# Cross attention with LayerNorm: row sums on VectorE, another order of the last tiles, x added by TensorE for the last two outputs

## The reference

```python
qs = (q @ wq).reshape(Bq, Lq, H, HD).transpose(0, 2, 1, 3)      # q is x
ks_ = (k @ wk)...; vs = (v @ wv)...                             # k and v are the context
scores = einsum('bhqd,bhkd->bhqk', qs, ks_) / sqrt(HD)
scores = where(mask, -inf, scores)
attn_w = softmax(scores, axis=-1)
out = (attn_w @ vs) @ wo + q
mu, var = mean(out), mean((out - mu) ** 2)
out = (out - mu) / sqrt(var + EPS) * gamma + beta
```

## Time and profile before

| | us |
|---|---|
| three runs, median (lowest to highest) | 640.73 (640.59 to 640.79) |
| the profiled execution | 641.83 |
| its span | 640.0 |
| TensorE busy, share of the span | 614.0, 96% |
| VectorE busy | 513.8, 80% |
| ScalarE busy | 523.8, 82% |
| POOL busy | 494.9, 77% |
| mean granted clock of TensorE, share of full speed | 0.991 |

### The profile page before, as it was taken

One profiled execution on the slowest core, in us unless ns is written; L12 is line 12 of the kernel. 1 busy time (PEld: TensorE's weight loads), 2 busy tenths in 40 slices (PEclk: granted clock), 3 DMA queues, 4 the chain that ended last, 5 costly groups with the idle time before them and its releaser, 6 DMA issues.

```text
span 640.0 us, 12593 instructions
## 1 busy us (share of the span) xinstructions
PE 614.0 (96%) x3816; PEld 485.2 (76%) x3816; DVE 513.8 (80%) x989; ACT 523.8 (82%) x1718; POOL 494.9 (77%) x639
## 2 busy tenths in 40 slices
PE   7988999999999999999999999999999999999885
PEld 5755687887878788787878878787878878786654
DVE  5844588888889888888879988887888988787787
ACT  4888998888878888897887988887988888789860
POOL 6475558797978979797987979797897879578674
PEclk9999899999999999999999999999999999999998
DMA  8450212222231232122231212232122221411103
GB/s 285 155 178 15 76 34 83 84 86 80 99 110 50 100 99 96 55 98 100 75 123 63 99 63 90 96 99 100 52 99 72 94 68 67 165 45 66 40 17 132
DMA packets 34786, 57.76 MB, mean 90 GB/s; under 512 B 6816, under 2 KB 7840, under 8 KB 34720
## 3 DMA queue, kind: packets, MB, share of 16 engines
q1 hardware_dynamic: 34720, 56.96, 26.4%
HBM read 39.53 MB, written 16.78 MB: 88 GB/s over the span
## 4 chain that ended last, share of the span: by engine, by line
PE 76%; DVE 10%; ACT 9%; issue 2%; SPq 1%; DMA 1%; POOLq 0%; POOL 0%; DVEq 0%; ACTq 0%
PE bank L384 24%; PE bank L308 22%; PE bank L331 14%; PE bank L341 7%; ACT pr L490 6%; PE bank L362 4%; DVE pr L628 2%; PE bank L367 2%; DVE nm L634 2%; PE bank L345 2%; PE bank L301 1%; DMA ptr<-xT 1%; DVE sm L642 1%; ACT ptr L456 1%; DVE kl L599 1%
## 5 line engine op out<-in xcount | busy, mean ns | idle before, releaser
L488 ACT ACTIVATE pr<-pr,nm 128x77 f32<-128x77 f32 x864 | 228.0, 347 | 52.3 <-DVE nm L634 50.3
L788 POOL TENSOR_TENSOR pn<-pr,rec 128x512 f32<-128x512 f32 x128 | 135.3, 1057 | 95.3 <-DVE rec L644 87.5
L628 DVE SCALAR_TENSOR_TENSOR pr<-msk,bank 128x308 f32<-128x308 uint8 x256 | 109.4, 469 | 41.2 <-PE bank L331 40.6
L634 DVE TENSOR_REDUCE nm<-pr 128x8 f32<-128x616 f32 x128 | 101.8, 795 | 4.4
L308 PE MATMUL bank<-xh,wqh 128*128 128x512 f32 x256 | 103.3, 403 | 1.3 <-DVE ql L616 1.3
L384 PE MATMUL bank<-woh,ah 128*128 128x512 f32 x256 | 101.8, 398 | 1.1 <-DVE al L651 1.1
L384 PE MATMUL bank<-woh,al 128*128 128x512 f32 x256 | 101.2, 395 | 0.0
L384 PE MATMUL bank<-wol,ah 128*128 128x512 f32 x256 | 101.1, 395 | 0.0
L308 PE MATMUL bank<-xh,wql 128*128 128x512 f32 x256 | 100.9, 394 | 0.0
L308 PE MATMUL bank<-xl,wqh 128*128 128x512 f32 x256 | 100.4, 392 | 0.0
L456 ACT ACTIVATE ptr<-bank 128x512 f32<-128x512 f32 (+1 forms) x256 | 95.3, 425 | 2.9 <-PE bank L341 2.8
(11 more groups left out here) (69 smaller groups left out, 1139.8 us busy)
## 6 DMA issues: line engine op xcount, KB each, us to landing
xraw<-xT SPq DMA_DIRECT2D x59, 256.0 KB, 3.0
xres<-x SPq DMA_DIRECT2D x58, 256.0 KB, 2.7
out<-y SPq DMA_DIRECT2D x56, 256.0 KB, 2.0
wk_sb<-wk SPq DMA_DIRECT2D x4, 256.0 KB, 4.1
wq_raw<-wq SPq DMA_DIRECT2D x4, 256.0 KB, 6.2
wv_sb<-wv SPq DMA_DIRECT2D x1, 1024.0 KB, 8.7
wo_raw<-xT SPq DMA_DIRECT2D x4, 256.0 KB, 8.8
wo_raw<-wo SPq DMA_DIRECT2D x1, 1024.0 KB, 5.4
```

The lines of the kernel that those rows point to most:

```text
L488: last = nc.scalar.activation(s, s, ACT.Exp, bias=nm[:, t % 2, h:h + 1], scale=1.0)
L628: nc.vector.scalar_tensor_tensor(out=pr[:, 4 * g:4 * g + 4, :], in0=msk[:, b % 2, t % TB, :].unsqueeze(1).broadcast_to([P, 4, LK]), scalar ...
L634: nc.vector.tensor_reduce(nm[:, t % 2, HH * half:HH * half + HH], pr[:, HH * half:HH * half + HH, :], AX.X, ALU.max, negate=True).then_inc ...
L788: nc.gpsimd.tensor_tensor(pn[:, half, 0:4, :].rearrange("p s (e k) -> p (s e) k", e=2), pr[:, hs, 0:KM], rec[:, t % 2, hs].unsqueeze(2).br ...
```

## The change

Three things are changed.

- `SUMS` is gone: in all tiles the exponentials have no accumulator, and `row_sums` on VectorE reduces the eight sums before it takes the reciprocals.
- The order of the last tiles is another one on all four computing engines. SyncE's program is as it was.
- For outputs 62 and 63 (`XADD = T - 2`) TensorE adds x: an fp32 matmul of x with the identity opens the accumulation in a bank, and the twelve matmuls of the output projection go on top of it. The banks are the two score banks SB, and the matmul waits until the last mask operation has read them and until x has arrived. `residual` of these outputs takes mean and variance straight from the bank, and `finish_1` reads the bank.

```diff
-SUMS = (6, T - 4)
+XADD = T - 2
...
-        misc += [("o", T - 10), ("o", T - 9), ("v", E - 3), ("o", T - 8), ("o", T - 7), ("o", T - 6), ("v", E - 2), ("o", T - 5),
-                 ("o", T - 4), ("v", E - 1), ("o", T - 3), ("o", T - 2), ("o", T - 1)]
+        misc += [("o", T - 10), ("o", T - 9), ("v", E - 3), ("o", T - 8), ("o", T - 7), ("o", T - 6), ("v", E - 2),
+                 ("o", T - 5), ("o", T - 4), ("o", T - 3), ("v", E - 1)]
+        def out_bank(o):
+            return SB[o % 2] if o >= XADD else misc_bank(("o", o))
...
+            def add_x(t):
+                pe.wait_ge(d_xe, 16 * (T - VFIN))
+                pe.wait_ge(v_st, NG * T - 1 + t % 2)
+                nc.tensor.matmul(out_bank(t)[:], ident[:], z_of(t), start=True, stop=False)
...
             project_o(T - 10)
             transpose_p(T - 5, 0)
             scores(T - 4, (2, 3))
+            scores(T - 3, (0, 1))
             project_o(T - 9)
             transpose_p(T - 5, 1)
-            scores(T - 3, (0, 1))
+            scores(T - 3, (2, 3))
             weigh_v(E - 3)
-            scores(T - 3, (2, 3))
+            scores(T - 2, (0, 1))
             transpose_p(T - 4, 0, after=E - 3)
             project_o(T - 8)
             transpose_p(T - 4, 1)
-            scores(T - 2, (0, 1))
             project_o(T - 7)
             transpose_p(T - 3, 0)
             scores(T - 2, (2, 3))
+            transpose_p(T - 3, 1)
             project_o(T - 6)
-            transpose_p(T - 3, 1)
             scores(T - 1, (0, 1))
+            scores(T - 1, (2, 3))
             weigh_v(E - 2)
             project_o(T - 5)
-            scores(T - 1, (2, 3))
             transpose_p(T - 2, 0, after=E - 2)
             transpose_p(T - 2, 1)
             project_o(T - 4)
+            add_x(T - 2)
+            add_x(T - 1)
             transpose_p(T - 1, 0)
+            project_o(T - 3)
             transpose_p(T - 1, 1)
             weigh_v(E - 1)
-            project_o(T - 3)
             project_o(T - 2)
             project_o(T - 1)
...
-                    if SUMS[0] <= t < SUMS[1]:
-                        last = nc.scalar.activation(s, s, ACT.Exp, bias=nm[:, t % 2, h:h + 1], scale=1.0)
-                    else:
-                        last = nc.scalar.activation(s, s, ACT.Exp, bias=nm[:, t % 2, h:h + 1], scale=1.0,
-                                                    accum_out=sm[:, t % 2, h:h + 1])
+                    last = nc.scalar.activation(s, s, ACT.Exp, bias=nm[:, t % 2, h:h + 1], scale=1.0)
...
-                if SUMS[0] <= t < SUMS[1]:
-                    nc.vector.tensor_reduce(sm[:, t % 2, hs], pr[:, hs, :], AX.X, ALU.add).then_inc(v_sum, 1)
-                    dve.wait_ge(v_sum, n - 2 * SUMS[0])
+                nc.vector.tensor_reduce(sm[:, t % 2, hs], pr[:, hs, :], AX.X, ALU.add).then_inc(v_sum, 1)
+                dve.wait_ge(v_sum, n)
...
+                if o >= XADD:
+                    nc.vector.bn_stats(st[:, e], out_bank(o)[:]).then_inc(v_bs, 1)
+                    dve.wait_ge(v_bs, o + 1)
+                    nc.vector.bn_aggr(mv[:, e], st[:, e]).then_inc(v_bn, 1)
+                    return
```

More of the change, by code:

```diff
@@ L370, in weigh_v @@
                     mm.then_inc(p_pv, 1)
+            def add_x(t):
+                pe.wait_ge(d_xe, 16 * (T - VFIN))
+                pe.wait_ge(v_st, NG * T - 1 + t % 2)
+                nc.tensor.matmul(out_bank(t)[:], ident[:], z_of(t), start=True, stop=False)
             def project_o(t):
                 r = t % 4
-                misc_free(pe, ("o", t))
-                o = misc_bank(("o", t))
-                n = 0
+                if t < XADD:
+                    misc_free(pe, ("o", t))
+                o = out_bank(t)
+                n = 0 if t < XADD else 1
                 if t == 0:
@@ L384, in project_o @@
                         last = nc.tensor.matmul(o[:], w[:, k, r * P:(r + 1) * P], s[:, k, :],
-                                                start=(n == 0), stop=(n == 3 * KT - 1))
+                                                start=(n == 0), stop=(w is al and i == KT - 1))
                         n += 1
@@ L563, in _ @@
             keep_pt(T - 6, 1)
+            exps(T - 4, 0)
             standardise(T - 11)
-            exps(T - 4, 0)
             keep_pt(T - 5, 0)
@@ L572, in _ @@
             keep_pt(T - 4, 0)
+            standardise(T - 10)
             exps(T - 3, 1)
+            keep_pt(T - 4, 1)
+            keep_pt(T - 3, 0)
+            exps(T - 2, 0)
             standardise(T - 9)
-            keep_pt(T - 4, 1)
-            exps(T - 2, 0)
-            keep_pt(T - 3, 0)
             exps(T - 2, 1)
@@ L583, in _ @@
             keep_pt(T - 2, 0)
-            exps(T - 1, 1)
             standardise(T - 7)
             keep_pt(T - 2, 1)
+            exps(T - 1, 1)
             keep_pt(T - 1, 0)
@@ L671, in finish_1 @@
                 dve.wait_ge(v_bn, o + 1)
-                nc.vector.scalar_tensor_tensor(out=y_of(o), in0=z_of(o), scalar=mv[:, slot(o), 0:1], in1=gam[:],
-                                               op0=ALU.subtract, op1=ALU.mult).then_inc(v_y, 1)
+                nc.vector.scalar_tensor_tensor(out=y_of(o), in0=z_of(o) if o < XADD else out_bank(o)[:],
+                                               scalar=mv[:, slot(o), 0:1], in1=gam[:], op0=ALU.subtract, op1=ALU.mult).then_inc(v_y, 1)
             def finish_2(o):
@@ L722, in _ @@
             mask_max(T - 3, 0)
+            mask_max(T - 3, 1)
             residual(T - 9)
             low_a(E - 3, (0, 1))
-            mask_max(T - 3, 1)
+            low_a(E - 3, (2, 3))
             row_sums(T - 3, 0)
-            low_a(E - 3, (2, 3))
+            residual(T - 8)
             row_sums(T - 3, 1)
             mask_max(T - 2, 0)
-            residual(T - 8)
             mask_max(T - 2, 1)
@@ L733, in _ @@
             residual(T - 7)
+            mask_max(T - 1, 0)
             row_sums(T - 2, 1)
-            mask_max(T - 1, 0)
             residual(T - 6)
             low_a(E - 2, (0, 1, 2, 3))
+            row_sums(T - 1, 0)
+            finish_1(T - 6)
+            residual(T - 5)
             mask_max(T - 1, 1)
-            row_sums(T - 1, 0)
-            residual(T - 5)
-            finish_1(T - 6)
+            finish_2(T - 6)
             row_sums(T - 1, 1)
-            finish_2(T - 6)
+            residual(T - 4)
             finish_1(T - 5)
-            residual(T - 4)
             finish_2(T - 5)
@@ L750, in _ @@
             residual(T - 3)
+            residual(T - 2)
             finish_1(T - 3)
-            residual(T - 2)
             finish_2(T - 3)
@@ L836, in _ @@
             normalise(T - 4, 0)
-            deviation(T - 10)
             normalise(T - 4, 1)
             gain_and_shift(T - 11)
+            deviation(T - 10)
+            normalise(T - 3, 0)
             deviation(T - 9)
-            normalise(T - 3, 0)
+            deviation(T - 8)
+            normalise(T - 3, 1)
             gain_and_shift(T - 10)
-            normalise(T - 3, 1)
-            deviation(T - 8)
             normalise(T - 2, 0)
+            deviation(T - 7)
             gain_and_shift(T - 9)
             normalise(T - 2, 1)
-            deviation(T - 7)
             deviation(T - 6)
+            gain_and_shift(T - 8)
             normalise(T - 1, 0)
+            normalise(T - 1, 1)
             deviation(T - 5)
-            normalise(T - 1, 1)
-            gain_and_shift(T - 8)
+            gain_and_shift(T - 7)
             deviation(T - 4)
-            gain_and_shift(T - 7)
             deviation(T - 3)
```

1 line of the change is left out of this document (removed).

## The result

The changed kernel takes **636.69 us** (median of nine executions, 635.37 to 639.87), the kernel before, beside it, 641.07 (nine, 640.59 to 642.3). The ratio is 0.9938, 95% interval 0.9917 to 0.996: faster by 4.0 us, between 2.6 and 5.3. That is inside the predicted range and 1.2 us above the forecast of 635.5. The profiled execution took 635.87 us around a span of 633.7, against 641.83 and 640.0 before.

What follows compares the result with a forecast made beforehand. TensorE, busy 96% of the span, was taken as the bound, with time to win only at its two ends. Head -4.0 and tail -1.2 gave -5.2 us: 635.5 us, range 634.0 to 636.5 (chance 0.50).

Steps and rivals of the forecast that it cites:

- The head: Tiles 0 to 5: row sums on VectorE save ScalarE 0.74 us a half tile; TensorE's last stall 4.0 us earlier.
- the 8.8 us taken as their latest landing: Head, value transfers: slowest kind takes 8.8 us, holding output 0 until 79.8 at most, 1.7 us lost; taken as none.
- the price of a fall in the head: TensorE's clock falling at the head's stall: score and projection matmuls lose 1.6 us, of which 0.9 is slack.
- one rival of 0.20: Head gives less: values land late or the clock falls at 62 us; head -2.4, time 637.1 us; chance 0.20.
- both should shift alike: Profiled execution (641.83 us) and median of the runs (640.73) were to move by the same -5.2 us.
- The tail: Last tiles: new order and x on TensorE give -1.2 us, 1.0 taken off for a clock fall; bounds -4.2 and +0.3.
- the two finishing operations: VectorE, outputs 59 and 60: collide with POOL, so the last subtraction starts 3.9 us after POOL's deviation, at 625.2 to 626.5.
- x on TensorE: Tail, outputs 62 and 63: two fp32 matmuls, at most 0.90 us each, stand in TensorE's waits and cost 0.
- The 0.3 us taken off at the end: Last deviation: 0.3 us less, as VectorE's mean subtraction reads the bank and no longer meets POOL in SBUF.
- The row sums did what they say: Rival on the head: VectorE's chain sets both halves, tiles 0.1 to 0.2 us worse, head +0.5, time 640.0; chance 0.11.
- The tail did not open fully: Rival on the tail: deviation and gain clear of finishing operations, clock holds; tail -4.2, time 632.5 us; chance 0.12.
- The rival on the slower side: TensorE's clock: each fall takes back 1.8 us of 6.2 won; gain gone from the fourth, 643.5 with five; chance 0.07.

Runs made afterwards that it cites:

- e1: Kernel before with the row sums of tiles 0 to 5 on VectorE too, last tiles as before: 637.13 us, ratio 0.9943.
- e12: Changed kernel with POOL's deviation of output 60 ahead of gain and shift of output 57, run for its trace: 637.69 us.
- e2: Kernel before with all row sums on VectorE and the old order of the last tiles: 641.12 us, ratio 0.9995.
- e3: Changed kernel with ScalarE's accumulator back for tiles 0 to 5 only: 639.18 us, ratio 0.9982.
- e4: Changed kernel with VectorE instead of TensorE adding x for outputs 62 and 63, which stay in the score banks: 638.85 us, ratio 0.9974.
- e10: Changed kernel with nine idle matmuls at tile 4, none in the tail: 635.82 us, ratio 0.9912.
- e6: Changed kernel with nine idle matmuls at tile 4 and five ahead of output 62: 635.61 us, ratio 0.9919.
- e11: Changed kernel with nine idle matmuls at tile 4 and POOL's deviation of output 60 ahead of gain and shift of output 57: 635.98 us, ratio 0.9913.
- e8: Changed kernel with ScalarE's accumulator for tiles 60 to 63 only: 637.76 us, ratio 0.9958.
- e5: Changed kernel unaltered, run once more on another chip: 635.99 us, ratio 0.9926.
- e7: Changed kernel with POOL's deviation of output 60 ahead of gain and shift of output 57: five executions 635.09 to 637.56 us, ratio 0.9922.

## Why the prediction was right, and where it was not

**The head was right in its steps.** Mask of tile 6 at 80.15 for 80.1 us, exponentials of tile 5 at 77.05 for 77.03, no stall after that, and e1 gives 3.7 to 4.0 us for 4.0. That the two times agree to 0.05 us is luck: the execution started 0.5 us late, so these steps were 0.5 us faster than forecast. The small value transfers did not hold output 0; the 8.8 us taken as their latest landing is a median, so that bound was not one. The stall at tile 4 was 1.53 us for 1.8. A second one, 0.88 us, was not foreseen: the next scores there wait for a low half of q behind tile 4's mask and maximum. It lies ahead of the point that the forecast rested on and cost nothing in it.

**The step that failed is the price of a fall in the head.** I had 1.6 us less 0.9 of slack, 0.7 net. e12 shows 1.5 for one fall, e2 2.9 for a longer one. There is no slack: between 64 us and the last stall TensorE never waits, and the last stall is 0.84 us with and without a fall. It is the round trip from TensorE's own transposes over ScalarE's copy and back, so it moves with TensorE and absorbs nothing. The kernel before, whose times do not rise with a lower clock (e1), seems to absorb its fall; the change took that away. The chance was too low as well. The fall had its place within one rival of 0.20; but 6 of 20 executions lost 1.9 us or more, and the median lies about a microsecond above the executions without a fall. At a clock of 0.999 the kernel takes 635.35 to 636.1.

**That 635.5 lies so near those is partly luck.** The sum was counted from the profiled execution and taken over to the median ("both should shift alike"). They did not: the profiled execution of before had a fall in its tail worth 1.1 us (e1), which is just the 1.1 by which it stood above 640.73, so it moved by 6.0 us (641.83 to 635.87) and the median by 4.4 (641.07 to 636.69). Against that the tail gave 1.5 us more than forecast (1.0 of it the fall that did not come), and the median of before was 0.3 higher beside the result. 635.5 + 1.1 + 0.3 - 1.5 is 635.4, the time without a fall; the rest up to 636.69 goes with the falls in the head, for which the sum had nothing, and with the scatter of the runs.

**The tail: order of events right, a size off.** On e3's clock, which is that of the prediction to 0.3 us, the bank waits are 0.31 and 0.56 us at 582.1 and 587.1 (0.3 at 582.3, 0.9 at 587.4), POOL's normalisation holds the transposes ahead of output 58 for 0.54 (0.7), and output 62 starts at 625.35 (626.3). I had strung the two finishing operations behind three POOL operations, 3.9 us on from a deviation's end. In the trace the pair takes 3.29 us from first start to the low half's (618.25 to 621.54), 3.4 from the deviation's end at 618.14, and that is why the low half comes at 625.2 on the clock of before, the early end of my bounds. The value matmuls also end later, at 620.6, which is 624.2 for 623.3 to 624.0. So TensorE idles 1.40 us for the 2.3 and more I expected, and the clock, for whose fall I had taken off 1.0 us, holds. Tail -2.7 us for -1.2, or for -2.2 without a fall. Of the 2.7, 1.1 is the fall that the profiled execution of before had in its tail (e1); against a tail without it the new one gains 1.6.

**x on TensorE** cost what was said, 0.86 us each (612.81 to 614.53 for two) where at most 0.90 was the bound, and nothing on the path. The 0.3 us taken off at the end came too: from the last statistics to the last operation it is 2.44 us (628.03 to 630.47) for 2.74 (634.03 to 636.77). What I missed is its use: without it TensorE idles 2.56 us instead of 1.40 before output 62 and the clock falls (e4), which makes a saving of 0.7 us one of 2.4. Reading a bank is free: the statistics take 0.69 us from PSUM and from SBUF alike. By the start costs that the Trainium skill gives ("VectorE: DVE Perf Modes", the section on the TRN2 errata) they should take 0.06 us longer, which is an estimate from its 120 cycles for PSUM and 58 for SBUF. The rows speak against it.

**The rivals.** The row sums did what they say (e1). The tail did not open fully: the finish met POOL's gain and shift, and its 1.69 and 1.75 us fell to 0.75 and 0.74 once they were apart (e12). The Trainium skill ("SBUF — State Buffer", "Who interferes with whom") says that a VectorE instruction with two SBUF inputs contends with a GpSimd instruction that reads SBUF, and the trace agrees. The rival on the slower side was not reached, though its mechanism is what spreads the executions. What the prediction had not seen at all is that the parts depend on each other. It listed the sums of the last tiles under neither head nor tail with a price of their own, and with the falls that come with them they cost 2.3 us in one order and gain 1.6 in the other.

**Best of all kernels run** is the changed one with nine idle matmuls at tile 4 (e10, 635.82 us; e6, 635.61, with five more in the tail; e11, 635.98): 5.5 to 5.6 us below the kernel before on its chip. The three can't be told apart, and their intervals overlap with the changed kernel's (0.9912 [0.9898, 0.9925] for 0.9922 [0.991, 0.9934] on one chip).

**Open:** what decides, in executions of one kernel, whether the clock falls after the stalls at 62 and 64 us. That filling them keeps it up has 0 of 14 against 9 of 26 executions above 637.3 us for it, but on one chip the unfilled changed kernel had none above it in five. The changed kernel's own executions above 637.3 us have no trace; that they have falls in the head is taken from e12, e2 and the clocks. Which part of e8's spread up to 642.89 is in its tail is not known either.

## What to carry to other kernels

Before a stall is counted as slack, ask who starts its chain: one that waits for a copy of TensorE's own last result moves with TensorE and absorbs nothing. Price the parts of a change in the order in which they will run, since the same sums, with the clock's falls, cost 2.3 us where VectorE is late and gain 1.6 where ScalarE is. And where TensorE idles a microsecond or two on its way into dense work, matmuls that cost nothing in an idle gap can be worth more than their result, because the work behind the gap then runs at 2.4 GHz.

## What the runs showed of the hardware that was not expected

*The clock as a lottery.* The changed kernel took 635.35 to 638.71 us on one chip (e5), at mean granted clocks from 0.999 to 0.992. Nine matmuls without a reader (2.1 us at 0.233 each), put into its idle time, cost nothing, and the 14 executions with them took 635.33 to 636.57 us.

*An execution at half speed.* One execution of e7 took 1234.46 us, its five others 635.09 to 637.56. The page of that execution (span; a group, total us, mean ns) and a window of it, columns as in the earlier trace rows:

```profile
span 1232.3 us, 12457 instructions
...
L311 PE MATMUL bank<-xh,wqh 128*128 128x512 f32 x256 | 178.8, 698 | 0.0
```

```profile
100.00:600.00 500.00, 499.27 (x1593) 335.49 (x1592) 222.22 (x417) 223.79 (x670) 205.29 (x268) 1.00 0.12 41
```

In the changed kernel the same group takes 402 ns a matmul for 698 here, and TensorE does 6.3 matmuls a microsecond (2912 in 460 us) for 3.2 here (1593 in 500). VectorE's sums are as fast as ever (778 ns for 780). The span nearly doubled, while the granted clock is recorded as 1.00 throughout, so the recorded clock doesn't tell of this. It was not seen in any other of the executions, and e12, the same program, took 637.69.
